# Ones for two pairs of banks from four row tiles at once, and one step moved on GpSimd and one on VectorE

## What is computed

```
xn  = group_norm(x);  q, k, v = split(w_qkv @ xn)          # 4 heads of 32
q   = elu(q) + 1;     k = elu(k) + 1
kv  = sum over tokens of k v^T;  k_sum = sum over tokens of k
out = (q kv) / (q . k_sum + 1e-6)
out = group_norm(w_out @ out) + x
```

## Time and profile before

| | us |
|---|---|
| median of 3 runs | 697.13 |
| lowest and highest | 695.99 and 697.78 |
| the profiled execution, whole | 694.95 |
| its span in the trace | 693.1 |

### The profile page before, as it was taken

The page is one execution under the profiler, slowest core; times in us unless marked ns, Lnnn a source line. Parts: engine busy times, 40 slices in busy tenths (PEclk is TensorE's granted clock), DMA queues, the critical chain, the costliest instruction groups (busy, mean ns, idle before and its releaser), DMA issues.

```text
span 693.1 us, 27323 instructions
## 1 busy us (share of the span) xinstructions
PE 635.0 (92%) x10484; PEld 537.4 (78%) x10484; DVE 570.9 (82%) x1951; ACT 461.3 (67%) x1061; POOL 136.7 (20%) x114
## 2 busy tenths in 40 slices
PE   4999999999999899999999999958999999999970
PEld 4899999888889799999999999935655555555540
DVE  4899998888888788989999999988777767767683
ACT  2565666999999856666656666666666776776641
POOL 0023000000000000000000000000327666666664
PEclk9999999999999999999999999989999999999995
DMA  9999760000000000000000000000532755746756
GB/s 173 204 203 201 152 134 0 2 0 0 0 0 0 1 2 0 0 0 0 0 2 0 0 0 0 0 1 2 122 79 78 158 105 122 170 88 126 159 90 122
DMA packets 63611, 43.27 MB, mean 62 GB/s; under 512 B 42000, under 2 KB 56144, under 8 KB 63568
## 3 DMA queue, kind: packets, MB, share of 16 engines
q1 hardware_dynamic: 60272, 41.89, 30.3%
q10 hardware_dynamic: 3296, 0.82, 0.7%
HBM read 33.39 MB, written 9.31 MB: 62 GB/s over the span
## 4 chain that ended last, share of the span: by engine, by line
DVE 31%; PE 30%; issue 13%; POOL 12%; ACT 7%; DMA 2%; DVEq 1%; ACTq 1%; POOLq 0%; SPq 0%
PE bank L479 21%; DVE scan_rows L743 9%; DVE parts L729 7%; DVE parts L743 7%; POOL rows_h L400 7%; DVE fin L802 3%; ACT cols_w L1090 3%; POOL fin L421 3%; ACT parts L1074 2%; PE bank L557 1%; PE bank L607 1%; ACT rows_h L1188 1%; POOL scale L404 1%; PE bank L531 1%; DVEq L743 1%
## 5 line engine op out<-in xcount | busy, mean ns | idle before, releaser
L479 PE MATMUL bank<-parts 128*128 128x124 f16 (+2 forms) x7560 | 434.4, 219 | 16.1 <-DVE parts L236 8.7
L479 PEld LDWEIGHTS bank<-parts 128*128 128x128 f16 x7560 | 418.4, 98 | 31.9 <-issue 12.1
L1074 ACT ACTIVATE parts<-parts 128x128 f16<-128x128 f16 x508 | 157.0, 309 | 126.7 <-DVE parts L743 104.8
L729 DVE TENSOR_TENSOR parts<-scan_rows,parts 128x128 f16<-128x128 f32 x508 | 149.5, 294 | 14.3
L743 DVE SCALAR_TENSOR_TENSOR parts<-bank,cols_w 128x128 f16<-128x128 f32 x378 | 109.6, 290 | 20.5 <-PE bank L479 7.3
L743 DVE SCALAR_TENSOR_TENSOR scan_rows<-bank,cols_w 128x128 f32<-128x128 f32 x378 | 105.9, 280 | 0.1
L1090 ACT ACTIVATE cols_w<-scan_rows 64x256 f32 (+1 forms) x128 | 82.7, 646 | 2.3
L389 POOL TENSOR_TENSOR scale<-dev,half 128x2 f32<-128x2 f32 (+1 forms) x2 | 2.1, 1038 | 414.0 <-DVE dev L827 414.0
L400 POOL TENSOR_TENSOR rows_h<-rows_h 128x512 f32<-128x512 f32 x56 | 69.8, 1279 | 32.8 <-DMA rows_h<-bounce 32.8
L869 DVE SCALAR_TENSOR_TENSOR kp<-ex,bank 128x512 f32<-128x512 f32 x64 | 40.9, 681 | 33.2 <-ACT ex L1168 33.0
L1082 ACT ACTIVATE cols_w<-scan_rows 128x256 f32 x126 | 52.5, 417 | 5.7 <-DVE scan_rows L743 0.3
(11 more groups left out here) (134 smaller groups left out, 559.1 us busy)
## 6 DMA issues: line engine op xcount, KB each, us to landing
rows_h<-bounce SPq DMA_DIRECT2D x56, 256.0 KB, 5.0
cols_w<-x SPq DMA_DIRECT2D x12, 896.0 KB, 13.6
out<-fin SPq DMA_DIRECT2D x12, 512.0 KB, 7.4
cols_w<-x SPq DMA_DIRECT2D x6, 640.0 KB, 10.9
cols_w<-x SPq DMA_DIRECT2D x6, 256.0 KB, 6.6
out<-rows_h SPq DMA_DIRECT2D x6, 256.0 KB, 4.7
bounce<-recip SPq DMA_DIRECT2D x14, 64.0 KB, 1.6
out<-rows_h ACTq DMA_DIRECT2D x2, 256.0 KB, 3.8
```

What stands on the lines that cost most here:

```text
L479: last = nc.tensor.matmul(conv_rows[g][u % SLOTS][:, :, to], w[:, k, d, :], rows_16[:, u % SLOTS, g * GB:(g + 1) * GB, of], start=part_n = ...
L729: nc.vector.tensor_tensor(low[:, slot, gb, :], state[:, slot, gb, :], high[:, slot, gb, :], ALU.subtract).then_inc(low_ready[g], 1)
L1074: act.activation(high_down[:, slot, gb, :], high[:, slot, gb, :], ACT.Copy, scale=1.0 / LOW_SCALE).then_inc(down_ready[g], 1)
```

## The change

There are three edits, and none alters the arithmetic.

1. Ones. `first_rows` gets its row of ones at four places, partitions 0, 32, 64 and 96. For chunks 0 to 2 the ones of both key banks and both query banks are written together at the head of `keys` by four matmuls of 32 rows each, in the order key 0, query 0, key 1, query 1. `keys` therefore also waits there for `qp_ready`, until VectorE has read the query banks of the chunk before. For chunk 3 the ones stay where they were, two matmuls for each pair, now 32 rows high.
2. GpSimd: the units of m=1 come right behind those of m=0, ahead of the power, scale and shift.
3. VectorE: at i=1 the copy of `mix` comes ahead of the two key banks.

```diff
-            for d in range(2):
-                nc.gpsimd.memset(first_rows[d * C:d * C + 1, :], 1.0).then_inc(cleared, 1)
-            pool.wait_ge(cleared, 3)
+            for d in range(4):
+                nc.gpsimd.memset(first_rows[d * DH:d * DH + 1, :], 1.0).then_inc(cleared, 1)
+            pool.wait_ge(cleared, 5)
...
                 if prev:
                     normalise_units(b, par, 0)
+                if prev:
+                    normalise_units(b, par, 1)
                 if pp:
 
                     at_least(pool, small_read, small_step(b, 5))
                     scale_and_shift(b, par)
-                if prev:
-                    normalise_units(b, par, 1)
...
+            def with_ones(banks, tiles):
+
+                for to, n in zip(banks, tiles):
+                    here = slice(n * DH, (n + 1) * DH)
+                    nc.tensor.matmul(to[:, :], first_rows[here, :], row_of_ones[here, :], start=True, stop=False)
+
             def keys(b, par, i):
 
                 at_least(pe, kp_ready, KBANKS * b + 2 * i)
-                for d in range(2):
-                    nc.tensor.matmul(key_ps[d][:, :], first_rows[rows_of[d], :], row_of_ones[rows_of[d], :],
-                                     start=True, stop=False)
+                if i < NCHUNK - 1:
+                    at_least(pe, qp_ready, UNITS * b + 2 * i)
+                    with_ones((key_ps[0], query_ps[0], key_ps[1], query_ps[1]), range(4))
+                else:
+                    with_ones(key_ps, (0, 2))
...
             def queries(b, par, i):
-                at_least(pe, qp_ready, UNITS * b + 2 * i)
-                for d in range(2):
-                    nc.tensor.matmul(query_ps[d][:, :], first_rows[rows_of[d], :], row_of_ones[rows_of[d], :],
-                                     start=True, stop=False)
+                if i == NCHUNK - 1:
+                    at_least(pe, qp_ready, UNITS * b + 2 * i)
+                    with_ones(query_ps, (1, 3))
...
                 for i in range(4):
+                    if i == 1 and prev:
+                        small(b, 2)
                     if cur:
                         keys(b, i)
...
-                    if i < 2 and prev:
-                        small(b, 2 * i)
+                    if i == 0 and prev:
+                        small(b, 0)
```

## The result

| | before | after |
|---|---|---|
| median, us | 696.58 (694.55 to 697.88, 12 runs) | 698.32 (696.04 to 700.68, 12 runs) |
| span of the profiled execution, us | 693.1 | 695.7 |

The ratio is 1.0031, 95% interval 1.0016 to 1.0046. By the ratio the kernel is 2.2 us slower (1.7 by the two medians), where 3.9 us faster was forecast. The median lies inside the range given, but on the other side of the kernel before.

The account below looks back on a forecast made before the run. Behind untouched scans, the loop's chain was taken to run over GpSimd, though TensorE is busiest. Image 0 +0.9, image 2 -1.1, four periods -5.2, tail +1.5 gave -3.9 us: median 697.13 to 693.2 us, 8-in-10 range 691.0 to 700.2.

Parts of the forecast that it names:

- GpSimd's move in the loop: Units of m=1 start up to 2.5 us earlier, alternate with VectorE's low part; TensorE's 0.30 and 0.47 us waits go.
- T: TensorE's first token matmul of the next image: forecast 17.46 us after an affine's start, next affine 7.15 us later.
- Mix copied first: TensorE's 0.80 us wait for mix goes; a new wait for query banks in keys leaves 0.58 us of it.
- Ones: Four 32-row ones on TensorE take 0.22 us, upper bound 0.44, saving 0.22 us in each of three chunks.
- Image 0: Ahead of the loop, the new wait for query banks delays chunk 2; image 1 starts 0.9 us later.
- Image 1: Ahead of the loop: nothing is won, as its outputs wait for DMAs; change 0.
- Image 2: Ahead of the loop: ones save 0.44 us and the first affine comes sooner; -1.1 us.
- The tail: Behind the loop, shift follows the units, delaying ScalarE's affine and last copy: +1.5 us, between +0.9 and +1.9.
- the lost race: Rival: GpSimd's shift loses to VectorE's normalise, so the period is 25.9 us and the kernel 699.5 us; chance 0.20.
- The low part did not starve: Rival denied here: VectorE's low part waits for all four units, period about 27.6 us, kernel 707 us; chance 0.05.
- hindered the units as forecast: Forecast: low part and GpSimd's units take turns; rival of less or no hindrance, 692.2 us, chance 0.12.
- That the row tiles gain nothing: Rival: four row tiles on TensorE are no faster than two pairs, about 0.3 us more in each of five, 694.7; chance 0.08.

Follow-up runs that it names:

- f1: Kernel before plus GpSimd's new order (old order kept in the last body) and mix copied first, without the ones edit: 690.75 us, ratio 0.9909.
- f2: Kernel before plus only the new wait for the query banks ahead of the key banks' ones, chunks 0 to 2: 697.57 us, ratio 1.0020.
- e1: Kernel before plus only the ones edit with its wait: 699.81 us, ratio 1.0047.
- e4: Changed kernel, but image 0 writes its ones in pairs with the old waits: 698.30 us, ratio 1.0032 to the kernel before.
- e6: Changed kernel with image 0's ones in pairs and GpSimd's old order in the last body: 694.07 us, ratio 0.9949 to the kernel before.
- g3: g1 and g2 combined: 689.85 us, ratio 0.9910 to the kernel before.
- f3: Kernel before with ones written by pairs of 32-row tiles in all four chunks, no new wait or grouping: 701.27 us, ratio 1.0073.
- e5: Changed kernel, but GpSimd keeps its old order in the last body: 692.79 us, ratio 0.9936 to the kernel before.
- f4: Changed kernel without the ones edit, GpSimd's new order in every body: 694.26 us, ratio 0.9967 to the kernel before.
- the two warmed kernels: Changed kernel and kernel before, each with ten extra matmuls ahead of image 0: 697.28 us (ratio 0.9999) and 695.68 us (ratio 0.9992).
- g2: f1 plus four ones at once in chunks 0 to 2 except image 0, 64-row pairs elsewhere: 691.05 us, ratio 0.9935 to the kernel before.
- g1: f1 plus VectorE waiting for the shift before its next normalise, from the third body on: 689.94 us, ratio 0.9910 to the kernel before.

## Why the prediction was wrong, point by point

In the profile 6.5 us lie between the forecast (-3.9) and what came (+2.6): the tail 2.4, image 1 2.2, image 0 1.8, the loop 0.6, and image 2 -0.4 with a rest of -0.1.

- **GpSimd's move in the loop**: right. The turns with the low part, power's 0.56 us, the end of the waits for units, T to affine 7.02 us (forecast 7.15). Alone it takes 0.86 us off each period.
- **Mix copied first**: right in mechanism, the remaining wait of 0.61 us too. Alone it takes 0.67 us off each period and is the best single edit. Together with edit 2 it gives 1.5 us a period (24.47 in f1's last three against 25.96).
- **Ones**: wrong. The step that failed is "Half of the array's rows gives a pair of tiles in the time of one, so I read these as four abreast", with 0.22 us taken for four. I had it from 32 instructions on 32-row tiles among themselves, which show how they overlap, not what it costs to enter and leave them. It is 0.33 us up to the next product, and the 32-row pairs of chunk 3, which my working did not mention at all, cost 0.2 us more. The upper bound of 0.44 covered the four but not the pairs. So T came at A+17.76 and the loop's sum was 0.6 us too good; without edit 1 a period is 0.35 us shorter.
- **Image 0**: the direction was right, the size not. I had one wait of 1.15 us with 0.25 given back; it is 1.40 us by f2, since the wait bites again in chunk 2 and chunk 3 gives nothing back. The other 1.3 us are the clock: before's profile had an early rise (0.5), after's a late one (0.84, against e1). No row gave me a way to forecast that, and as one execution of each it says little of the medians.
- **Image 1**: forecast 0, profile +2.2. The step that failed is "nothing is won: its outputs wait for DMAs", which took the DMAs to keep their time and left out that later units meet the low part. SyncE's queue in the changed kernel, the first bounce of image 1 and the first gather behind it:

```profile
489.84 0.35 SPq L325 DMA_DIRECT2D bounce<-recip  x1
492.98 1.29 SPq L331 DMA_DIRECT2D rows_h<-bounce  x3
```

  The gathers went out 3.14 us behind the bounce, where before it was 2.10, so that GpSimd's units of m=0 start 18.01 us into the image and not 16.75. That is close enough to the low part for it to get in ahead of the last unit. GpSimd before, then GpSimd, VectorE and TensorE in the changed kernel:

```profile
496.65 4.98 POOL L400 TENSOR_TENSOR rows_h<-rows_h 128x512 f32<-128x512 f32 x4 [9.15 <-DMA rows_h<-bounce]
...
500.55 5.94 POOL L400 TENSOR_TENSOR rows_h<-rows_h 128x512 f32<-128x512 f32 x4 [10.29 <-DMA rows_h<-bounce]
...
503.73 3.84 DVE L259 TENSOR_TENSOR parts<-yn,parts 128x1024 f16<-128x1024 f32 x2
...
503.20 1.08 PE L614 MATMUL bank<-rows_h,mix 128*64 128x512 f32 x4 [1.43 <-POOL rows_h L400]
...
506.63 1.08 PE L614 MATMUL bank<-rows_h,mix 128*64 128x512 f32 x4 [0.92 <-POOL rows_h L400]
```

  The four units took 5.94 us in place of 4.98, and TensorE's outputs waited twice. Over all profiles image 1 lies between 22.88 and 26.96 us, and the traces show two sources. One is this meeting: from the token products of chunk 3 to those of image 2 it is 9.8 to 10.4 us in the five profiles in which the units started at most 3.7 us ahead of the low part (the changed kernel, e1, e4, e6, g3), and 7.8 to 8.4 us in the twelve in which they started 3.9 us or more ahead. The other is the clock: chunk 0 took 5.6 or 5.7 us in the five profiles in which it stayed at 2.4 GHz (before, the changed kernel, e1, f2, f3), and 6.4 to 7.8 us in the twelve in which it was at 1.2 GHz for a part. The late meeting came in five of the eight kernels with four ones at once and in none of the nine others. Whether edit 1 delays the bounce or chance did is open: the gap between bounce and gather lies between 1.63 and 3.25 us, and f3, without grouping, had 2.70. A transfer of instructions lies near the bounce in some of the profiles; nothing was run to test it.
- **Image 2**: -1.49 for -1.1, right.
- **The tail**: the step that failed is "Their gathers land at A+16.9", which I had carried over from the loop. They came at A+18.1 (657.31-639.17), which makes +2.35 of +1.5; my bound of +1.9 was too tight. The terms written there add up to A+25.7, too, and not to A+25.8. SyncE's queue in the last body, before and with the change:

```profile
650.39 1.73 SPq L331 DMA_DIRECT2D rows_h<-bounce  x4
...
649.34 1.73 SPq L331 DMA_DIRECT2D rows_h<-bounce  x4
```

  They were issued at A+10.17 (649.34-639.17), and in the tail before already at A+10.01 (650.39-640.38), where the loop has A+9.28. That is 0.9 of the 1.2 us, and the trace of before had it. And I had not asked what a TensorE that waits 2.6 us longer does to its clock: another 1.57 us. The tail's term I forecast at 1.5, and it is 3.9. e5 shows that it alone decides the sign.
- **The rivals**: the lost race is real. It did not come in the profile of the changed kernel, whose shift was 0.30 us or more ahead, but once in each of three kernels near it (e5, f1, f4). These periods are 1.1 to 1.6 us longer than their neighbours, where I had 1.3; 1.0 to 1.1 us of it is the longer shift, the rest units that began late. The low part did not starve, and it hindered the units as forecast. That the row tiles gain nothing was the rival nearest to the truth for the loop, and it still had the tiles too cheap. The changed kernel's 698.32 us lie near the forecast of the lost race, 699.5, by chance: that race was not lost in its profile.

## What to carry to other kernels

An order that is right for the steady loop is not for its last body: there nothing covers the step that comes late, and here undoing one move in the last body alone turned a loss of 0.3% into a gain of 0.6%. Matmuls that are cheap in a group of their own kind are not cheap between others: cost the entry and the exit, read where the sizes meet. And before giving an engine's bank a second condition, look at the image in which nothing else makes that engine wait.

## What the runs showed of the hardware that I had not expected

- Passing between row tiles of 64 and of 32 rows costs TensorE 0.10 us each way at 2.4 GHz (f3), and none is seen from a product over all 128 rows to 32-row ones (598.20 to 598.76 in f3, 0.56 us, as before's 0.55 to 64-row ones).
- TensorE's clock fell to 1.2 GHz after idle times of 3.24 to 3.79 us near the end (four kernels) and not after 2.94 us; in image 1 it fell in twelve executions and not in five, behind nearly the same idle time of 2.5 to 2.7 us. After the token products of image 0 began it rose between 3.2 and 9.8 us later, and between 3.2 and 6.0 us later in kernels that do the same work there as before (the two warmed kernels left out).
- A GpSimd instruction on one column, 0.34 us alone, takes 1.33 to 1.42 us if it starts between 0.14 us behind and 0.12 us ahead of a VectorE `tensor_scalar` over 2048 fp32 columns, and 0.34 us if it starts 0.21 us ahead or more (g2's first period has the 0.21). g1 makes that order certain with one wait.
- GpSimd's units and VectorE's low part take turns. The low part beside four units cost GpSimd 1.0 us in image 1 (5.94 for 4.98) and 1.1 us in the loop (6.04 for 4.97).
